# Two recurrent layers on one core: the scan and the feed forward offset by half rows, the wavelets in two parts

## The reference, cut to what matters

```
x  = input                                  # 4 rows x 1024 positions x 256 channels
xn = layernorm(x)                           # layer 0
s  = layernorm(xn + wavelet_attention(xn))  # 2 levels of 4-tap convolutions down, linear
                                            # attention over all 256 low positions, 2 levels up
g  = silu(ffn(xn))                          # silu(x W1) * (x W2); gelu(h H1); gelu(h H2); W3
x  = x + s * g
xn = layernorm(x)                           # layer 1
delta = softplus(xn Wd + bd);  Bm, Cm = xn Wbc + bbc
h[t] = exp(delta[t] A) * h[t-1] + delta[t] Bm[t] xn[t]   # 16 states a channel, along the row
y = sum over states(h * Cm) + D * xn;  o = x + y
s = gelu(layernorm(o) W1 + b1) W2 + b2 + o
g = silu(experts(x))                        # gate: top 2 of 8; all 8 experts are computed
x = x + s * g
```

## Time and profile before

| | us |
|---|---|
| median of 3 runs | 1715.9 (1714.0 to 1716.29) |
| the profiled execution | 1717.27 |
| its span | 1715.5 |
| PE busy | 1417.5 (83%) |
| DVE busy | 1403.9 (82%) |
| ACT busy | 1056.9 (62%) |
| POOL busy | 983.7 (57%) |

### The profile page before, as it was taken

The page is one execution under the profiler, slowest core; times in us unless marked ns, Lnnn a source line. Parts: engine busy times, 40 slices in busy tenths (PEclk is TensorE's granted clock), DMA queues, the critical chain, the costliest instruction groups (busy, mean ns, idle before and its releaser), DMA issues. The chain is left out here.

```text
span 1715.5 us, 16410 instructions
## 1 busy us (share of the span) xinstructions
PE 1417.5 (83%) x5229; PEld 623.9 (36%) x5296; DVE 1403.9 (82%) x1736; ACT 1056.9 (62%) x1514; POOL 983.7 (57%) x616
## 2 busy tenths in 40 slices
PE   4989989898998779898998779898998764555787
PEld 1444434434443334443443334443443321111333
DVE  2672369999889979999879979989879978999954
ACT  3536478768536668778536768777536753564654
POOL 3152255666208975766307975766307964786675
PEclk9999999999999999999999999999999975686989
DMA  8001000000101000000100100000100300000000
GB/s 196 12 5 57 1 13 1 4 22 1 74 13 36 27 25 1 0 26 0 74 13 19 43 25 1 1 26 1 74 13 2 133 25 0 0 1 0 1 13 12
DMA packets 12599, 42.42 MB, mean 25 GB/s; under 512 B 1866, under 2 KB 1890, under 8 KB 10466
## 3 DMA queue, kind: packets, MB, share of 16 engines
q1 hardware_dynamic: 11698, 35.08, 5.6%
q0 software_dynamic: 816, 6.30, 1.7%
HBM read 38.23 MB, written 4.19 MB: 25 GB/s over the span
## 5 line engine op out<-in xcount | busy, mean ns | idle before, releaser
L773 POOL TENSOR_TENSOR gx<-gx,sy 128x1024 f32<-128x1024 f32 x120 | 295.0, 2459 | 52.3 <-DVE sy L2245 46.3
L796 POOL TENSOR_TENSOR gate<-gate,lin 128x512 f32<-128x512 f32 x120 | 153.0, 1287 | 255.0 <-DVE lin L2365 245.2
L911 ACT ACT_TABLE_LOAD x189 | 242.5, 1283 | 43.0 <-PE psf L1479 20.7
L1501 PE MATMUL psf<-g1p,h2w 128*128 128x512 f16 x768 | 177.6, 379 | 4.1 <-ACT tf L979 3.6
L2212 DVE TENSOR_TENSOR psu<-so,psu 128x1024 f32<-128x1024 f32 x128 | 156.6, 1224 | 21.2 <-PE psu L1625 11.2
L1105 ACT ACTIVATE da<-delta,aneg 128x512 f32<-128x512 f32 x256 | 163.7, 710 | 9.3 <-DVE st L2229 8.8
L751 POOL TENSOR_TENSOR g2p<-tf,g2p 128x512 fp32r<-128x512 f32 x64 | 93.4, 1466 | 120.6 <-ACT g2p L1002 120.2
L2229 DVE TENSOR_TENSOR_SCAN st<-da,carry,psu 128x512 f32<-128x512 f32 x128 | 156.8, 1266 | 2.0 <-ACT carry L1120 0.2
L2229 DVE TENSOR_TENSOR_SCAN st<-da,psu 128x512 f32<-128x512 f32 x128 | 149.0, 1205 | 1.5
L801 POOL TENSOR_TENSOR ap<-gate,ap 128x512 f16<-128x512 f32 x116 | 143.3, 1254 | 3.8 <-ACT ap L1212 3.8
L1204 ACT ACTIVATE gate<-gate 128x512 f32<-128x512 f32 x128 | 77.6, 623 | 73.8 <-DVE gate L2354 73.1
(11 more groups left out here) (372 smaller groups left out, 3059.5 us busy)
## 6 DMA issues: line engine op xcount, KB each, us to landing
mw<-in_mlp_w SPq DMA_DIRECT2D x3, 2048.0 KB, 8.0
xn<-in_x SPq DMA_DIRECT2D x8, 512.0 KB, 7.0
wf<-in_wf SPq DMA_DIRECT2D x4, 1024.0 KB, 4.8
xr<-in_x SPq DMA_DIRECT2D x8, 512.0 KB, 4.0
x<-gx SPq DMA_DIRECT2D x8, 512.0 KB, 3.8
out<-outc SPq DMA_DIRECT2D x8, 512.0 KB, 3.1
mw<-in_mlp_w SPq DMA_DIRECT2D x3, 1024.0 KB, 10.1
h1w<-in_h POOLq DMA_DIRECT2D x1, 2048.0 KB, 12.5
```

The costliest lines, as they stand in the source:

```text
L773: pool.tensor_tensor(out, chunk(gx, c), sy[:, n % 2], ALU.add).then_inc(y_acc.sem, 1)
L796: pool.tensor_tensor(gate[:, r % NG], gate[:, r % NG], lin_at(b, r)[:], ALU.mult)\
L911: act.preload_act_table_set(name)
L1501: last = pe.matmul(banks[m], w[:, t, cols], src[:, half, t], start=(t == 0 and half == 0), stop=(t == KF - 1 and half == 1))
```

## The change

Every order is written anew. The same arithmetic is done, half a row apart:

- opening: feed forward of half (0, 0), the wavelets of row 0, the head of (0, 0); then the feed forward of half (0, 1) beside the scan of half (0, 0).
- turn(row), for rows 0 to 2, has four stages. A: norm, hidden and experts of half (row, 0), beside the first part of the wavelets of row + 1 (46 of 88 steps) and the head of (row, 1). B: feed forward of half (row + 1, 0) beside the scan of (row, 1). C: norm, hidden and experts of half (row, 1), beside the second part of the wavelets (42 steps), `lb_*` of both halves and the head of (row + 1, 0). D: feed forward of half (row + 1, 1) beside the scan of (row + 1, 0).
- closing: norm and experts of half (b, 0) beside the head and the scan of (b, 1), then the experts of half (b, 1).

Between the two parts of the wavelets three intermediates (`h1b`, `h2b`, `low2`; 2060 words of a partition, about 1.05 MB) go to DRAM by one DMA and come back by another. `wf1`, `mw1` and `mw2` are loaded for each half, twice a row. The gate's choice and weights run for each half, 26 small DVE instructions each. The eight copies of the residual (x2 from gx) are gone: `l0_out` writes `x2` itself. `delta`, `nrm`, `nf`, `bcs` and `combs` have one buffer instead of one for each half, and `xn1` lies in `so`. POOL takes the odd states only in the last row's half 1; its half 0 has the states 4, 6 and 8 there. By count of the written orders ACT changes its table 226 times instead of 187.

```diff
+KEPT = ((0, L // 2 + 2), (KD * (L // 2 + 2), L // 4 + 2), (KD * (L // 2 + L // 4 + 4), L // 4 + 2))
+KEPT_WORDS = KD * (L + 6)
+MADE, DONE = 46, 88
...
-            return n in (TAIL_STEPS[c] if tail(b) else MIDDLE_STEPS)
+            return n in (TAIL_STEPS if tail(b) and c == 1 else MIDDLE_STEPS)
...
+        spill = nc.dram_tensor("spill", (P, KEPT_WORDS), F32).ap()
...
-        nf = r2("nf", 14336, [P, NC, KD, N], BF16)
+        nf = r2("nf", 14336, [P, KD, N], BF16)
...
+            def spill_waves(b):
+                sp.wait_ge(conv.sem, conv.at(b, MADE))
+                sp.dma_start(spill, wave.kept[:]).then_inc(kept_out.sem, 16)
+            def fetch_waves(b):
+                sp.wait_ge(kept_out.sem, kept_out.at(b - 1, 1))
+                sp.wait_ge(g1_mm.sem, g1_mm.at(b, KF))
+                sp.dma_start(wave.back[:], spill).then_inc(kept_in.sem, 16)
...
             def turn(row):                       # the SP queue
-                load_hidden(row - 1)
-                load_experts(row - 1)
-                for c in range(NC):
-                    load_residual(row, row, c, wave)
-                if row == B - 1:
-                    load_tail(row)
-                if row + 1 < B:
-                    load_x(row + 1, row + 1)
-                store_out(row - 1, row - 1, True)
+                load_x(row + 1)
+                load_hidden(row, 0)
+                load_experts(row, 0)
+                load_residual(row, 1, wave)
+                spill_waves(row + 1)
+                store_out(row, 0)
+                load_hidden(row, 1)
+                fetch_waves(row + 1)
+                load_experts(row, 1)
+                load_residual(row + 1, 0, wave)
+                store_out(row, 1)
...
             def l0_out(b, c, w):
-                pool.tensor_tensor(chunk(gx, c), chunk(gx, c), w.xr[:], ALU.add).then_inc(x2n.sem, 1)
+                pool.tensor_tensor(chunk(x2, c), chunk(gx, c), w.xr[:], ALU.add).then_inc(x2n.sem, 1)
...
+                if w is wave:
+                    dve.wait_ge(kept_in.sem, kept_in.at(b - 1, 1))
+                low2, h2b, h1b = (w.low2_in, w.h2b_in, w.h1b_in) if w is wave else (w.low2, w.h2b, w.h1b)
...
-            def expert_choice(b, part=0):
+            def expert_choice(b, part):
                 step = gate_steps(b, part * GATE_STEPS)
...
     # PE, turn(row) from the end of stage B to that of C (only its norm, hidden and first experts)
+                lf_average(row, 1); ffn_half(row + 1, 0, 22, 0)
+                ffn_half(row + 1, 0, 23, 0); lf_variance(row, 1); ffn_half(row + 1, 0, 22, 1)
+                ffn_half(row + 1, 0, 23, 1); project(row + 1, 0, 6); project(row + 1, 0, 7); expert_mean(row, 1)
+                hidden1(row, 1, 0); hidden1(row, 1, 1); expert_logits(row, 1); hidden2(row, 1, 0)
+                hidden1(row, 1, 2); hidden2(row, 1, 1); hidden1(row, 1, 3); expert_turn(row, 1)
```

More of the change, by code:

```diff
@@ L489, in build @@
         layer = 1
-        le_copy = [sig(f"le_copy{c}", 1, 16) for c in range(NC)]
         le_mean = sig("le_mean", NC)
@@ L896, in _ @@
             l0_low(0, 0)
             opening()
-            for row in range(1, B):
-                turn(row, row == B - 1)
+            for row in range(B - 1):
+                turn(row, row == B - 2)
             closing(B - 1)
@@ L1044, in lb_affine @@
                     part = w.y0[:, t, c * N:(c + 1) * N]
-                    last = act.activation(part, part, ACT.Identity, scale=col("gamma", t), bias=col("beta", t))
+                    out = part if c == 0 else gx[:, t, c * N:(c + 1) * N]
+                    last = act.activation(out, part, ACT.Identity, scale=col("gamma", t), bias=col("beta", t))
                 last.then_inc(lb_norm.sem, 1)
@@ L1098, in decay @@
                     act.wait_ge(head_done.sem, head_done.at(b, c + 1))
-                if k == 0:
-                    act.wait_ge(p1_mm.sem, p1_mm.at(b - 1, Q))
+                    if not (tail(b) and c == 1):
+                        act.wait_ge(p1_mm.sem, p1_mm.at(b, c * NQ))
                 act.wait_ge(scan_done.sem, scan_done.at(b, KD * (k - 3)))
                 for t in range(KD):
-                    last = act.activation(da[:, n % 4, t], delta[c][:, t], ACT.Exp, scale=aneg[:, t, n:n + 1])
+                    last = act.activation(da[:, n % 4, t], delta[:, t], ACT.Exp, scale=aneg[:, t, n:n + 1])
                 last.then_inc(da_done.sem, 1)
```

1491 lines of the change are left out of this document (730 added, 761 removed).

## The result

The changed kernel takes 1702.0 us (median of 4 runs, 1701.22 to 1704.8) against 1715.6 before: ratio 0.9925, 95% interval 0.9908 to 0.9942, so 0.75% faster. Predicted were 1700 and 0.9%. The profiled execution has a span of 1700.2 us.

A forecast was written before the change was run, and what follows sets the result against it. No engine's total bound the kernel: DVE led the scan stages, PE and then POOL the others, with both ends poor. Opening 260 + three turns of 400 + closing 240 gave about 1700 us, 0.9% faster, range 1650 to 1750.

The forecast's parts named there:

- one of its own signs: The prediction called itself wrong if the closing saved less than 60 us or DVE was busy below 86% of a turn.
- Closing: From the end of the scan of (3, 0) to the span's end: 240 us against 314.7 before, 225 to 252.
- Opening: Up to the end of the scan of half (0, 0): first input at 172, 260 us in all against 229.6 before.
- Turn: Each of three turns: 400 us against 390.4 before; scan stages 197 and other stages 200 by the old busy shares.
- The high end of my range, 414: A turn with 5 us of added work, 11.3 of waits at a second stage start and 7.7 at `expert_sum`.
- The gate's second pass: In each turn, 26 more small DVE instructions of 0.19 us add 5 us of DVE work.
- Table loads: ACT: 39 more by written orders, 50 us, beside DVE's work except one load each in the norm's and head's chains.
- Transfers: Second weight loads, spill and fetch cost nothing in the sum; 10 us each if their cover is gone.
- (1): Every half's norm, logits, choice and last down projection waited for in full: turn 414, total 1747 us, slower; chance 0.20.
- (2): Added work falls into DVE's idle time: turn 391, closing 230, opening 258, total 1661 us; chance 0.18.
- (3): The clock falls in stages A and C, each of six stages losing 5 us: 1730 us; chance 0.09.
- (4): In each turn a late second load of `mw` or the fetch holds DVE or PE by 12 us: 1736; chance 0.06.

The follow-up runs named there:

- e1: Changed kernel with the closing's residual load of half (3, 1) issued ahead of the tail's weight loads: 1693.7 us, ratio 0.9873 to the kernel before.
- e2: Changed kernel with the scan norm's average and square put earlier, at the end of stage D, for rows 1 and 2: 1696.6 us, ratio 0.9886 to the kernel before.
- e4: Changed kernel with 15 of the gate's 26 small VectorE instructions left out in each half row: 1697.4 us, ratio 0.9892 to the kernel before.
- e8: Changed kernel with ScalarE going through two other table sets before the roots' set at scan norm and head, 38 more loads: 1744.1 us, 39 us more.
- e3: Changed kernel with a second, needless load of the roots' table set at both norms and the head, 24 by count: 1707.4 us, 4 us more.
- e5: Changed kernel with each added transfer (second weight loads, spill, fetch) made twice, the second after the first landed: 1703.7 us, ratio 0.993 to the kernel before.
- e10: Changed kernel with 40 needless GpSimd products of 128x192, all in SBUF, at the start of each turn: 1733.4 us, 29 us more.
- e7: Changed kernel with both the earlier residual load in the closing and the earlier norm for rows 1 and 2: 1687.0 us, ratio 0.9833 to the kernel before.

## Why the prediction was right, step by step

The total is right within 2 us and the terms within 13, but the pieces inside the terms are off by up to 34 us and cancel. By one of its own signs the prediction was wrong: VectorE was to be busy at least 86% of a turn, and it was busy 83.9%, 85.4% and 83.1%.

*Closing (240, measured 243.1).* The right term, from two errors. The scan from first input to end took 98.7 us with VectorE busy 98.03; I had 117 for it, which is 107 us of work at the old share of 91.7%. The head's chain ahead of it took 61.4 and not 41: 7 to 8 us are the residual input behind the tail's weights (e1), the rest the feed forward's end, gate and product of half (3, 1), which end 14 us after the scan that they ran beside. I started this chain as if the row's input were there. Before the last scan's end VectorE had 124.3 us of work in all, where I had counted 145. The tail took 83.0, as predicted, though with 50.3 us of VectorE in it and not 41.3.

*Opening (260, measured 246.8).* The first input came at 166.8 (I had 172): the centring came at 135.3 and not 132, but the chain from it took 31.6 us and not 41. The scan took 80.0 us and not 90: VectorE was busy 77.82 us there, where I had counted 84 (6.6 of the 10 us), and its share was 97%, where I had scaled by 93.1%.

*Turn (400, measured 403.4).* The sum is right and the split is not. In turn 1 the scan stages took 172.5 us, predicted 197, and stages A and C 233.6, predicted 200. Two steps failed, and they offset each other.

In the scan stages it was mainly the count of work. I had 183.3 us for VectorE and it had 164.95, which at the old share is 20 of the 24 us; the share rose from 93.1% to 95.6%, the other 5. Of the 18 us of work, 4.3 are my window's: it ran to 440, the last scan had ended at 435.6. Another 7.6 are `g1p`, 11.6 us in a turn instead of 19.2 (see below); the rest is not separated.

In A and C it was the scaling by the old busy share. The work was as counted (175.7, I had 171.5), but the share fell from 85.6% to 75%, because they now start twice, and e2 shows that such a start is time in the open. The high end of my range, 414, priced that from the waits; I counted half of it as refilled. What paid it back was the shorter scan stages, not order at the boundary. A turn came out near 400 because VectorE had 14 us less to do than I had counted and was idle 65 us instead of 42.

*The gate's second pass (5 us a turn).* Present on VectorE, worth nothing in the turns (e4).

*Table loads (in the shares).* 36 more in the trace, 39 by the written orders. Turn 1 has 55 loads instead of 45, stages A and C 28 of them where the same work had 19. At e8's 1.0 us each, the 10 more would be 10 of the 13 us that a turn lost; the single ones that e3 added in stages A cost nothing. So this stays open between 0 and 10. The Trainium skill (ScalarE: Activation LUTs, What ACT_TABLE_LOAD costs) gives 1.38 us of drain on top; the trace does not agree: three loads in a row start 1.29 us apart, the activation 1.29 behind the last.

*Transfers.* All that the change added are hidden, as predicted (e5). The one that was not hidden is one that it only moved. I had written that a load which waits for a scan's end holds those behind it, and had looked for it in the turns alone.

*The rivals.* (1) is right in its mechanism and wrong in its size: the waits for the norms and the sum are 29.8 us on DVE in turn 1 against 13.4, and the starts of the stages take 38 us more, but the scan stages paid it back. (2) did not come. (3) is there in part: clock 0.91 in stages A of turns 1 and 2, and a wait for four float32 matmuls is 1.6 to 1.9 us longer at the lower level. What it costs in all is not measured; the 3.3 us that e2 won there are order. (4) came in the closing, 7 to 8 us once and not 12 in every turn.

*VectorE's 37 us.* Not foreseen. In the kernel before, `g1p` (L2017, all operands in SBUF) was slow where GpSimd ran beside it. Groups of DVE by form, before and after:

```profile
L2017 DVE SCALAR_TENSOR_TENSOR g1p<-tf,g1p 128x512 f16<-128x512 f32 x64 | 67.4, 1070 | 21.4 <-ACT g1p L997 21.3
...
L2198 DVE SCALAR_TENSOR_TENSOR gx<-so,pk,gx 128x512 f32<-128x512 f32 x8 | 18.9, 2395 | 0.0
...
L2198 DVE SCALAR_TENSOR_TENSOR gx<-xn,pk,xc 128x512 f32<-128x512 f32 x6 | 9.1, 1552 | 0.0
```

```profile
L1981 DVE SCALAR_TENSOR_TENSOR g1p<-tf,g1p 128x512 f16<-128x512 f32 x64 | 44.9, 727 | 3.9 <-ACT g1p L977 3.9
...
L2164 DVE SCALAR_TENSOR_TENSOR gx<-so,pk,gx 128x512 f32<-128x512 f32 x16 | 16.5, 1073 | 0.0
```

22.5 us less for the one, and for the other 28.0 for 14 of its 16 before against 16.5 for all 16. Both kernels do the same operations. Of the 64 `g1p` 18 took 0.97 us or more before and 4 after, the others 0.66 to 0.79, which fits new orders that put fewer of them beside GpSimd. That a GpSimd instruction beside them is what stretches them is shown by e10; that it explains the whole difference is not.

## What to carry to other kernels

A finer pipeline trades the ends for more stage starts: price each start from its waits in full, and for the stage that it empties count the work anew, from its own instructions, before scaling by a share. After a reorder, read every queue for what now stands ahead of a small transfer: here swapping two lines of the SyncE queue gave 9 us and moving one norm ahead of two projections 7, beside 13 from the whole change; the same move where TensorE was not late cost 3. An instruction added to an engine with idle time in that stage can cost nothing (the gate in the turns, a single table load at the head) or most of its length (three loads in a row there): its place decides, not the engine's total.

## What the runs showed of the hardware

- A VectorE instruction with all operands in SBUF ran at 1.07 us instead of 0.74 beside GpSimd products of 128x192, and in the kernel before 2.46 instead of 0.68 beside GpSimd sums of 128x1024; one that reads PSUM did not change (1.22). The two instructions before in the fences below:

```profile
1158.43 5.10 POOL L773 TENSOR_TENSOR gx<-gx,sy 128x1024 f32<-128x1024 f32 x2
```

```profile
1159.17 4.91 DVE L2017 SCALAR_TENSOR_TENSOR g1p<-tf,g1p 128x512 f16<-128x512 f32 x2
```

The Trainium skill (SBUF — State Buffer, SBUF: two separate sides) has a rule that fits: a VectorE instruction with two SBUF inputs and a GpSimd instruction that reads SBUF take one pair of ports in turn, each for its whole length. The trace agrees in direction, 0.68 becoming 2.46 beside a sum of 2.55; the rule was not weighed in the prediction.

- A table load takes 1283 ns, three in a row too, and also when its set is already there and other activations have run since (10 such in e3). One written directly behind a load of the same set left no record (14 in e3).
- The granted clock of stage A of turn 0, in one and the same order, was 0.97 in e7 and 0.95 in e2, and the stage 110.1 and 111.7 us long. The difference is four float32 matmuls, the norm's variance, which took 1.98 us in one and 3.57 in the other.
